# The output stage's row sums, reciprocals and first two batches prepared inside the attention stage, in GpSimd pieces of 512 columns

## The chip, the cores and the metric

One core of a Trainium2 chip runs the whole program in one launch. The metric is the device time of that launch in microseconds (us). The engines are TensorE (PE in the profile; PEld is its weight load), VectorE (DVE), ScalarE (ACT), GpSimd (POOL) and SyncE (SP), which here only issues DMA transfers.

## The reference

Four residual layers over x (4 batches x 512 rows x 512 columns), in float32:

```python
x = x + tanh(g_xattn[0]) * L0_xattn(layernorm(x), ctx, mask)         # one head, 1024 context rows
x = x + tanh(g_ffn[0])   * L0_ffn(layernorm(x), router, wg, wu, wd)  # 8 experts, quantized, top 1
x = x + tanh(g_xattn[1]) * L1_xattn(layernorm(x), ctx, Wq..bo)       # 16 heads of 32
x = x + tanh(g_ffn[1])   * L1_ffn(layernorm(x), w1, b1, w2, b2)      # 8 experts x 64 rows per batch
```

The change lies in the third layer. For each batch and each of 16 heads: scores = Q K^T / sqrt(32), softmax over 1024 context rows, context = softmax V; then `context @ Wo.T + bo`, the gate, the residual, and the layernorm and transposition that the last layer needs.

## The kernel before

The program is a row of stages, each a block of five instruction streams (one for each engine) with a barrier behind it: context, readout, router, mixture, query, attention, output, expert. Matmul operands are split into two bf16 halves (high and low), whose products are added up.

**Attention** (`attention_phase`) goes over 4 batches x 16 heads x 4 quarters u of 256 context rows; a quarter of a head is called a step here, 64 to a batch. The batch's step number is 4h+u. At a step TensorE issues eight matmuls of 512 columns: two that find a row maximum of a step 28 steps ahead (L1706, into `psM`, two slots), two for the scores 4 steps ahead (L1725), four that mix the values of this step (L1736). ScalarE takes the exponentials of those scores (L1632). Their low halves, 128x1024, are made by GpSimd for u = 0 and 2 (L1591) and by VectorE for u = 1 and 3 (L1678). VectorE also takes the maxima (L1670), so two steps of it are one low half and two maxima. The last batch has no maxima left to find from its step 36 on (head 9), and TensorE then has six matmuls a step. Once in 16 steps, at step number 5 modulo 16, GpSimd splits the maxima into three bf16 parts with four small instructions (`max_parts`, L1601 to L1607); TensorE transposes them four steps later (L1714) into a slot of `psM`. `copy_out` (L1646) takes a head's 96x512 sums, and SyncE stores them to `mixed_dram` (L1568): in it are, for each batch, two partial contexts (r = 0, 1) and the row sums of the softmax (r = 2).

**Output** (`output_phase`) does this for each batch of 128x2048 numbers: load both partial contexts (`load`, L1812), add them (L1900 on VectorE for batches 0 and 1, L1858 on GpSimd for 2 and 3), multiply by the reciprocal row sums (L1905), add the bias and split into halves (`high` L1868 on ScalarE, low L1908 on VectorE), project with Wo (L1970), update the residual `xres` and take statistics (L1915 to L1924), 1/sqrt on GpSimd (L1853), normalise (L1931), split (L1876, L1937), transpose (L1982), copy to `xeT` (L1881, L1943). The reciprocals need a way round: the row sums of all batches are loaded (L1821), inverted (L1949), stored to `rsum_dram` (L1827), and loaded again, each repeated over 32 partitions (`load_rsums`, L1817). GpSimd first adds the gated bias `bob` to all 16 rows of `xres` (L1848). VectorE goes through the batches in the order update, normalise, low half, divide(b+2), copy.

Everything on an engine runs in the order written; nothing is scheduled by a tool. Work on an engine waits for semaphores only, so the order within each stream is what the change moves.

## Time and profile before

| | us |
|---|---|
| median of 3 runs | 1772.18 (1770.33 to 1776.66) |
| the profiled execution | 1772.23, its span 1770.4 |
| attention, until the last copy of a head ends | to 1278.4 of the span |
| output stage, first DMA to last copy | 1284.84 to 1405.9 |
| expert stage | 1406 to the end |

The page's line for the span in 40 slices shows TensorE busy at nine tenths in attention (slices 20 to 28), at 2 and 6 to 5 tenths in the three slices after it, which are the output stage, and at nine tenths again in the expert stage:

```text
PE   4999988999551774878999999999826599999996
```

Times in the trace count from the span's start. A row of the timeline tells start, length, engine, line and operation, and in brackets how long the engine sat idle before it and what ended that. Several equal instructions in a row are merged, with their count behind an x.

### The profile page before, as it was taken

What the parts mean: (1) busy time and instruction counts of PE and PEld (TensorE: products, weight loads), DVE (VectorE), ACT (ScalarE), POOL (GpSimd) and SP (SyncE); (2) the same over time, 40 slices, a digit from 0 to 9 for tenths busy, and PEclk for the clock granted to TensorE, in tenths of its full rate; (3) what the DMA queues carried; (4) which work ended last, traced back from release to release, by engine and by line L of the source; (5) the groups of instructions that cost most, each with busy time, mean ns of one, the idle gap of its engine ahead of it and who ended that gap; (6) DMA issues with size and microseconds to landing.
All of it is one profiled execution on the core that took longest, in us unless ns stands there. A gap on an engine that the chain in (4) does not pass through costs nothing. (4 is left out here: it accounts for less than half of the span.)

```text
span 1770.4 us, 24758 instructions
## 1 busy us (share of the span) xinstructions
PE 1454.6 (82%) x8465; PEld 839.6 (47%) x8536; DVE 1258.1 (71%) x1520; ACT 970.7 (55%) x1440; POOL 438.6 (25%) x343
## 2 busy tenths in 40 slices
PE   4999988999551774878999999999826599999996
PEld 3554534555240333323555555555403366666663
DVE  4888856655582676859999999999448686655551
ACT  5878723344171555414777777767612376665551
POOL 0122210000313004304555555555752000000000
PEclk9999998999755996878999999999958699999998
DMA  6788650000083226420423233331177396666640
GB/s 220 244 276 290 204 205 1 0 0 0 1 354 111 72 90 186 111 79 11 97 74 95 76 92 79 90 81 28 36 213 226 115 327 219 219 220 219 220 142 28
DMA packets 145938, 236.92 MB, mean 134 GB/s; under 512 B 11320, under 2 KB 61496, under 8 KB 144704
## 3 DMA queue, kind: packets, MB, share of 16 engines
q1 hardware_dynamic: 140352, 210.65, 38.5%
q0 software_dynamic: 5504, 25.20, 3.9%
q8 instruction: 48, 0.79, 0.2%
q14 instruction: 34, 0.28, 0.1%
HBM read 169.74 MB, written 59.59 MB: 130 GB/s over the span
## 5 line engine op out<-in xcount | busy, mean ns | idle before, releaser
L1632 ACT ACTIVATE t_e<-t_psE 128x512 f32<-128x512 f32 x512 | 304.6, 597 | 133.6 <-PE t_psE L1725 124.9
L1670 DVE TENSOR_REDUCE t_nmax<-t_psM 128x1 f32<-128x1024 f32 x256 | 301.5, 1212 | 15.7 <-PE t_psM L1706 15.6
L1591 POOL TENSOR_TENSOR t_low<-t_e 128x1024 bf16<-128x1024 f32 x128 | 250.0, 1955 | 196.4 <-ACT t_e L1632 186.7
L1736 PE MATMUL t_psO<-t_e,vst 128*96 128x512 bf16 x512 | 200.6, 392 | 2.4 <-POOL t_low L1591 2.4
L1725 PE MATMUL t_psE<-qst,kst 99*128 99x512 bf16 x512 | 195.2, 382 | 0.1
L1736 PE MATMUL t_psO<-t_low,vst 128*96 128x512 bf16 x512 | 193.1, 377 | 0.0
L1678 DVE TENSOR_TENSOR t_low<-t_e 128x1024 bf16<-128x1024 f32 x128 | 177.9, 1390 | 18.3 <-ACT t_e L1632 17.8
L1706 PE MATMUL t_psM<-kst,qst 96*128 96x512 bf16 x512 | 164.0, 404 | 28.0 <-DVE t_nmax L1670 22.7
L2218 PE MATMUL e_psG<-xeT,e_w1p 128*128 (+1 forms) x1536 | 172.8, 276 | 9.4 <-DVE e_hT L2162 4.8
L2218 PEld LDWEIGHTS e_psG<-xeT,e_w1p 128*128 128x128 bf16 x1536 | 151.7, 99 | 30.9 <-issue 5.9
L2233 PE MATMUL e_psO<-e_w2p,e_hT 128*128 128x512 bf16 x752 | 164.9, 379 | 0.8
L2233 PEld LDWEIGHTS e_psO<-e_w2p,e_hT 128*128 128x128 bf16 x768 | 75.1, 98 | 88.9
L1736 PEld LDWEIGHTS t_psO<-t_e,vst 128*96 128x96 bf16 x512 | 84.1, 164 | 64.8 <-POOL t_low L1591 6.0
L1736 PEld LDWEIGHTS t_psO<-t_low,vst 128*96 128x96 bf16 x512 | 84.4, 165 | 27.4
L1706 PEld LDWEIGHTS t_psM<-kst,qst 96*128 96x128 bf16 x512 | 47.4, 99 | 94.0 <-DVE t_nmax L1670 47.2
L2114 ACT CAST e_w2p<-xres 128x2048 bf16<-128x2048 f32 x32 | 60.7, 1898 | 53.1 <-PE e_psO L2233 35.2
L642 PE MATMUL a_psR<-ctxN,a_pT 128*128 (+1 forms) x375 | 85.7, 384 | 4.3 <-DVE xres L555 3.9
L620 PE MATMUL a_psS<-ctxT,a_xT 128*128 (+1 forms) x375 | 87.8, 389 | 0.6 <-issue 0.2
L358 PE MATMUL c_psG<-ctxT,c_wT 128*128 128x512 bf16 x369 | 86.8, 383 | 1.0 <-issue 0.2
L115 POOL DMA_DIRECT2D ternary<-c_wout x48 | 41.7, 868 | 185.0 <-ACT c_wout L228 185.0
L2120 ACT ACTIVATE e_g<-e_psG,e_b1T 128x256 f32<-128x256 f32 x128 | 53.7, 470 | 59.5 <-PE e_psG L2218 40.7
L361 PE MATMUL c_psG<-c_wT,ctxT 128*128 128x512 bf16 x371 | 85.6, 379 | 0.7
(229 smaller groups left out, 2309.3 us busy)
## 6 DMA issues: line engine op xcount, KB each, us to landing
piece<-in_L_ffn_w SPq DMA_DIRECT2D x32, 1024.0 KB, 13.5
xres<-in_L_ffn_w SPq DMA_DIRECT2D x32, 1024.0 KB, 15.2
wT<-ternary POOLq DMA_DIRECT2D x8, 1536.0 KB, 21.4
kst<-keys SPq DMA_DIRECT2D x96, 128.0 KB, 4.2
mixed<-t_ost SPq DMA_DIRECT2D x64, 192.0 KB
c_rows<-in_ctx SPq DMA_DIRECT2D x8, 1024.0 KB, 10.3
xres<-in_L_ffn_wg SPq DMA_DIRECT2D x8, 1024.0 KB, 7.6
xres<-in_L_ffn_wu SPq DMA_DIRECT2D x8, 1024.0 KB, 7.1
```

What stands on the lines that cost most here:

```text
L358: last = nc.tensor.matmul(psG[:, k, :], wT[:, 0, a, k * P:(k + 1) * P], ctxT[:, b, q * 512:(q + 1) * 512], start=(i == 0), stop=(i == 11))
L620: last = nc.tensor.matmul(psS[:, par, h * 512:(h + 1) * 512], xT[:, par, ra * KC + k, :], ctxT[:, rb * KC + k, bass.ds(b * T + h * 512, 512)],
L642: last = nc.tensor.matmul(psR[:, :], pT[:, par, ra * TC + k, :], ctxN[:, bass.ds(b * TC + k, 1), rb, :].rearrange("p o d -> p (o d)"), sta ...
L1591: nc.gpsimd.tensor_tensor(low[:, slot(h, u), :, :], e32[:, slot(h, u), :, :], upper(h, u), ALU.subtract).then_inc(lo_pool, 1)
L1632: nc.scalar.activation(e32[:, slot(h, u), i, :], psE[:, i, :], ACT.Exp, scale=SC).then_inc(expd, 1)
L1670: nc.vector.tensor_reduce(nmax[:, h // G % 2, h % G, u:u + 1], banks_of(place_of_max(b, m)).rearrange("p a t -> p (a t)"), AX_X, ALU.max, ...
L1678: nc.vector.tensor_tensor(low[:, slot(h, u), :, :], e32[:, slot(h, u), :, :], upper(h, u), ALU.subtract).then_inc(lo_dve, 1)
L1706: last = nc.tensor.matmul(banks_of(place_of_max(b, m))[:, i, :], qst[0:KR, g, h % G, u * P:(u + 1) * P], kst[0:KR, g, h % G, i * 512:(i + ...
L1725: nc.tensor.matmul(psE[:, i, :], kst[:, g, h % G, k * P:(k + 1) * P], qst[:, g, h % G, :], start=True, stop=True).then_inc(scored, 1)
L1736: last = nc.tensor.matmul(psO[0:VW, h % 2, :], vst[:, g, 2 * u + i, :].rearrange("p (w h) -> p h w", h=G)[:, h % G, :], part[:, i, :], sta ...
L2218: last = nc.tensor.matmul(psG[:, g % 4, i, :], w1p[:, ra, k, f:f + P], xeT[:, rb * KC + k, ee, :].rearrange("p o s -> p (o s)"), start=(n ...
L2233: last = nc.tensor.matmul(psO[:, m, :], hT[:, ra, k, m * P:(m + 1) * P], w2p[:, rb, k, :], start=(k == 0 and i == 0), stop=(k == FC - 1 an ...
```

## The change

- **Batches 0 and 1 of the output stage** (PRE = 2) are prepared during the last batch of attention. SyncE loads their parts before the stores of heads 3 and 4; GpSimd adds the halves in eight pieces of 128x512, one behind each odd step of heads 4 to 7 (`add_halves`), and multiplies by the reciprocals in eight pieces behind each odd step of heads 9 to 12 (`divide`).
- **Reciprocals of batches 0 to 2**: sums loaded before the store of head 2, inverted by VectorE at step 20 of the last batch (48x512), stored before head 6's store, loaded repeated before those of heads 7 and 8. Batch 3's sums (16x512) stay in the output stage.
- **The gated bias**: loaded in batch 0, gated by VectorE at the start of batch 1, added to `xres` by GpSimd in 16 pieces of 128x512, at step numbers 5 and 13 modulo 16 of batches 1 and 2 (`bias_residual`).
- **The output stage** starts with `high` and `low` of batches 0 and 1. GpSimd adds the halves of batches 2 and 3 before its first 1/sqrt. Batches 2 and 3 have their own buffers.
- **Memory**: one allocation `prebob` holds the new buffers; the router's, query's and expert's tiles that were separate (`disp`, `qw32`, `xT`, `xeT`, `b2b`) are views of it.

The diff, cut to what the prediction speaks of:

```diff
+                def prepare_output(h):                                   # SyncE, last batch
+                    if h == 2:
+                        for i in range(2):
+                            sp.wait_ge(stored[i], 16 * (LAST * NH // 2 + 1))
+                        for b in range(LAST):
+                            load_sums(sp, b, o.sums[b * NH:(b + 1) * NH, :], mixed_dram, o.sums_loaded)
+                    if h in (3, 4):
+                        load_parts(sp, h - 3, o.pre[:, h - 3, :, :, :], mixed_dram, o.pre_loaded[h - 3])
+                    if h == 6:
+                        sp.wait_ge(o.rsums_ready, 1)
+                        sp.dma_start(o.rsum_dram[0:LAST].rearrange("b h s -> (b h) s"),
+                                     o.sums[:, :]).then_inc(o.rsums_stored, 16)
+                    if h in (7, 8):
+                        sp.wait_ge(o.rsums_stored, 16)
+                        sp.wait_ge(o.added, KC * (h - 6))
+                        load_rsums(sp, h - 7, o.pre[:, h - 7, 1, :, :], o.rsum_dram, o.rsum_loaded[h - 7])
...
                         if due := group_at(b, h, u, SPLIT_AT):            # GpSimd
                             max_parts(*due)
+                        if b in (1, 2) and h % 2 == 1 and u == 1:
+                            bias_residual((b - 1) * NH // 2 + h // 2)
+                        if b == LAST and 4 <= h < 8 and u % 2 == 1:
+                            add_halves((h - 4) // 2, (h % 2) * 2 + u // 2)
+                        if b == LAST and 9 <= h < 13 and u % 2 == 1:
+                            divide((h - 9) // 2, (h - 9) % 2 * 2 + u // 2)
...
+                    nc.gpsimd.tensor_tensor(o.xres[:, t, :], o.xres[:, t, :], o.bob[:, :], ALU.add).then_inc(o.biased, 1)
...
+                    pool.wait_ge(o.pre_loaded[b], 32)
+                    nc.gpsimd.tensor_tensor(o.pre[:, b, 0, k, :], o.pre[:, b, 0, k, :], o.pre[:, b, 1, k, :],
+                                            ALU.add).then_inc(o.added, 1)
...
+                    pool.wait_ge(o.rsum_loaded[b], 16 * (P // HD))
+                    pool.wait_ge(o.added, b * KC + k + 1)
+                    nc.gpsimd.tensor_tensor(o.pre[:, b, 0, k, :], o.pre[:, b, 0, k, :], o.pre[:, b, 1, k, :],
+                                            ALU.mult).then_inc(o.divided, 1)
...
+                def prepare_output(b, h, u):                              # VectorE
+                    if (b, h, u) == (1, 0, 0):
+                        dve.wait_ge(o.consts_loaded, 32)
+                        nc.vector.tensor_scalar(o.bob[:, :], o.bob[:, :], o.gates[:, 1:2], None, ALU.mult).then_inc(o.gated, 1)
+                    if (b, h, u) == (LAST, 5, 0):
+                        dve.wait_ge(o.sums_loaded, 16 * LAST)
+                        nc.vector.reciprocal(o.sums[:, :], o.sums[:, :]).then_inc(o.rsums_ready, 1)
...
+                load_sums(sp, LAST, sums[:, :], mixed_dram, sums_loaded)   # output stage, SyncE
+                for b in range(PRE, B):
+                    load_parts(sp, b, parts[:, b - PRE, :, :, :], mixed_dram, parts_loaded[b - PRE])
+                sp.wait_ge(rsums_ready, 1)
+                sp.dma_start(o.rsum_dram[LAST], sums[:, :]).then_inc(rsums_stored, 16)
+                sp.wait_ge(rsums_stored, 16)
+                for b in range(PRE, B):
+                    sp.wait_ge(added, b - PRE + 1)
+                    load_rsums(sp, b, parts[:, b - PRE, 1, :, :], o.rsum_dram, rsum_loaded[b - PRE])
...
-                pool.wait_ge(bo_gated, 1)                                 # output stage, GpSimd
-                for t in range(NT):
-                    nc.gpsimd.tensor_tensor(xres[:, t, :], xres[:, t, :], bob[:, :], ALU.add).then_inc(biased, 1)
+                for b in range(PRE, B):
+                    p = parts[:, b - PRE, :, :, :].rearrange("p r c s -> p r (c s)")
+                    pool.wait_ge(parts_loaded[b - PRE], 32)
+                    nc.gpsimd.tensor_tensor(p[:, 0, :], p[:, 0, :], p[:, 1, :], ALU.add).then_inc(added, 1)
...
-                divide(0)                                                 # output stage, VectorE
-                divide(1)
+                low(0)
+                low(1)
+                dve.wait_ge(sums_loaded, 16)
+                nc.vector.reciprocal(sums[:, :], sums[:, :]).then_inc(rsums_ready, 1)
```

GpSimd's stream over 16 steps of the last batch, before: eight low halves stand between two splits of the maxima.

```order
L1601 TENSOR_TENSOR t_nparts<-t_nmax,t_nparts 128x16
L1603 TENSOR_TENSOR t_nrest<-t_nmax,t_nparts 128x16
L1605 TENSOR_TENSOR t_nparts<-t_nrest,t_nparts 128x16
L1607 TENSOR_TENSOR t_nparts<-t_nrest,t_nparts 128x16
L1591 TENSOR_TENSOR t_low<-t_e 128x1024 x11
```

The same place after (`prebob` with L1690 is `divide`; the rows go on in this way up to the eighth piece and then `x4` low halves):

```order
L1649 TENSOR_TENSOR t_nparts<-t_nmax,t_nparts 128x16
L1651 TENSOR_TENSOR t_nrest<-t_nmax,t_nparts 128x16
L1653 TENSOR_TENSOR t_nparts<-t_nrest,t_nparts 128x16
L1655 TENSOR_TENSOR t_nparts<-t_nrest,t_nparts 128x16
L1690 TENSOR_TENSOR prebob<-prebob 128x512
L1639 TENSOR_TENSOR t_low<-t_e 128x1024
L1690 TENSOR_TENSOR prebob<-prebob 128x512
L1639 TENSOR_TENSOR t_low<-t_e 128x1024
```

A piece of 128x512 now stands ahead of each of seven low halves in the part of the batch that has no maxima, and the first stands between the split and the next low half. In batches 1 and 2 the pieces on `xres` are two for each eight low halves, the first again behind the split:

```order
L1655 TENSOR_TENSOR t_nparts<-t_nrest,t_nparts 128x16
L1680 TENSOR_TENSOR xres<-xres,prebob 128x512
L1639 TENSOR_TENSOR t_low<-t_e 128x1024 x4
L1680 TENSOR_TENSOR xres<-xres,prebob 128x512
L1639 TENSOR_TENSOR t_low<-t_e 128x1024 x4
```

VectorE around the start of the output stage, before (the first rows of the stage):

```order
L1678 TENSOR_TENSOR t_low<-t_e 128x1024 x13
L1550 UNCONDITIONAL_BRANCH
L1893 UNCONDITIONAL_BRANCH
L1947 TENSOR_SCALAR o_bob<-o_bob,gates 128x512
L1949 RECIPROCAL o_sums<-o_sums 64x512
L1900 TENSOR_TENSOR o_parts<-o_parts 128x2048
L1905 TENSOR_TENSOR o_parts<-o_parts 128x2048
L1908 SCALAR_TENSOR_TENSOR o_cpair<-o_parts,o_bias,o_cpair 128x512 x4
```

and after:

```order
L1749 TENSOR_TENSOR t_low<-t_e 128x1024 x13
L1573 UNCONDITIONAL_BRANCH
L1953 UNCONDITIONAL_BRANCH
L1965 SCALAR_TENSOR_TENSOR o_cpair<-prebob,o_bias,o_cpair 128x512 x8
L2006 RECIPROCAL o_sums<-o_sums 16x512
L1972 SCALAR_TENSOR_TENSOR xres<-o_psG,gates,xres 128x512
```

The sums, the four full-width instructions of batches 0 and 1 and the gating are gone from in front of the low halves; a reciprocal stands between the low halves and the first update.

## Rows read from the trace of the kernel before

**Rows 1.** Windows, busy us and (count) by engine, then clock, DMA share, GB/s.

```profile
1050.00:1160.00 110.00, 104.84 (x478) 61.68 (x477) 106.25 (x90) 78.14 (x137) 63.82 (x46) 1.00 0.36 89
1240.00:1278.00 38.00, 35.35 (x153) 20.93 (x151) 20.68 (x12) 29.43 (x54) 32.01 (x16) 1.00 0.14 37
1278.00:1406.00 128.00, 57.73 (x316) 30.18 (x320) 84.66 (x116) 27.42 (x41) 38.35 (x23) 0.71 0.56 170
```

**Rows 2.** Timeline of the output stage, by start: SyncE, VectorE, TensorE.

```profile
1284.84 1.95 SPq L1821 DMA_DIRECT2D o_sums<-mixed  x4
...
1292.38 3.34 DVE L1949 RECIPROCAL o_sums<-o_sums 64x512 f32<-64x512 f32 x1
...
1310.34 2.29 DVE L1905 TENSOR_TENSOR o_parts<-o_parts 128x2048 f32<-128x2048 f32 x1 [10.72 <-DMA o_parts<-rsum]
...
1318.78 21.97 PE L1970 MATMUL o_psG<-woT,o_cpair 128*128 128x512 bf16 x94 [40.98 <-DVE o_cpair L1908]
...
1323.64 2.74 DVE L1908 SCALAR_TENSOR_TENSOR o_cpair<-o_parts,o_bias,o_cpair 128x512 bf16<-128x512 f32 x4 [0.79 <-ACT o_cpair L1868]
```

**Rows 3.** Timeline of attention, GpSimd, just behind a split of maxima and in the repeating part.

```profile
1214.35 1.89 POOL L1591 TENSOR_TENSOR t_low<-t_e 128x1024 bf16<-128x1024 f32 x1
...
1226.06 1.89 POOL L1591 TENSOR_TENSOR t_low<-t_e 128x1024 bf16<-128x1024 f32 x1 [1.63 <-ACT t_e L1632]
1229.58 1.89 POOL L1591 TENSOR_TENSOR t_low<-t_e 128x1024 bf16<-128x1024 f32 x1 [1.63 <-ACT t_e L1632]
```

**Rows 4.** The same stretch on VectorE and TensorE.

```profile
1215.76 1.57 DVE L1678 TENSOR_TENSOR t_low<-t_e 128x1024 bf16<-128x1024 f32 x1
1217.24 1.21 DVE L1670 TENSOR_REDUCE t_nmax<-t_psM 128x1 f32<-128x1024 f32 x1
...
1220.67 1.23 DVE L1678 TENSOR_TENSOR t_low<-t_e 128x1024 bf16<-128x1024 f32 x1 [0.28 <-ACT t_e L1632]
...
1225.44 2.34 DVE L1670 TENSOR_REDUCE t_nmax<-t_psM 128x1 f32<-128x1024 f32 x2
1227.71 1.32 DVE L1678 TENSOR_TENSOR t_low<-t_e 128x1024 bf16<-128x1024 f32 x1
...
1218.51 0.60 PE L1706 MATMUL t_psM<-kst,qst 96*128 96x512 bf16 x2 [1.32 <-DVE t_nmax L1670]
...
1227.33 0.59 PE L1706 MATMUL t_psM<-kst,qst 96*128 96x512 bf16 x2
```

**Rows 5.** Line L1848, GpSimd's add of 128x512: minimum, median, maximum in ns.

```profile
L1848 POOL TENSOR_TENSOR xres<-xres,o_bob x16: 1255/1256/3315, 1292.5 to 1315.4; 128x512 f32<-128x512 f32 x16
```

**Rows 6.** Timeline of attention's last steps, without maxima: GpSimd, VectorE, TensorE.

```profile
1252.45 7.60 POOL L1591 TENSOR_TENSOR t_low<-t_e 128x1024 bf16<-128x1024 f32 x3 [1.16 <-DVE t_low L1678]
1261.22 7.60 POOL L1591 TENSOR_TENSOR t_low<-t_e 128x1024 bf16<-128x1024 f32 x3 [1.16 <-DVE t_low L1678]
...
1258.32 4.06 DVE L1678 TENSOR_TENSOR t_low<-t_e 128x1024 bf16<-128x1024 f32 x2 [1.87 <-ACT t_e L1632]
...
1275.78 0.47 PE L1736 MATMUL t_psO<-t_e,vst 128*96 128x512 bf16 x1 [0.82 <-POOL t_low L1591]
```

**Rows 7.** Timeline of the output stage, VectorE and GpSimd, one batch after another.

```profile
1326.29 0.74 DVE L1915 SCALAR_TENSOR_TENSOR xres<-o_psG,gates,xres 128x512 f32<-128x512 f32 x1
...
1333.59 6.12 DVE L1931 TENSOR_SCALAR o_xn<-xres,o_mom,o_rstd 128x512 f32<-128x512 f32 x4 [1.20 <-POOL o_rstd L1853]
...
1333.70 4.81 POOL L1858 TENSOR_TENSOR o_parts<-o_parts 128x2048 f32<-128x2048 f32 x1
...
1350.46 0.74 DVE L1915 SCALAR_TENSOR_TENSOR xres<-o_psG,gates,xres 128x512 f32<-128x512 f32 x1
...
1374.61 0.74 DVE L1915 SCALAR_TENSOR_TENSOR xres<-o_psG,gates,xres 128x512 f32<-128x512 f32 x1
...
1381.90 1.92 DVE L1931 TENSOR_SCALAR o_xn<-xres,o_mom,o_rstd 128x512 f32<-128x512 f32 x4 [1.20 <-POOL o_rstd L1853]
```

**Rows 8.** DMA issues from 1150 to 1410 us: KB each, median us from issue to landing.

```profile
o_parts<-mixed SPq DMA_DIRECT2D x8, 1024.0 KB, 8.3
```

More of the change, by code:

```diff
@@ L1 @@
+from collections import namedtuple
 from contextlib import ExitStack
@@ L1433, in _, with load_parts, load_rsums, load_sums @@
                     gemm(b)
-def attention_phase(nc, queries_dram, keys_dram, values_dram, mixed_dram, ident, qst, loaded, kst, vst, kv_loaded, ones_set):
+Output = namedtuple("Output", "pre sums bob bias rsum_dram gates xres bv bo consts_loaded sums_loaded pre_loaded rsum_loaded "
+                              "gated rsums_ready rsums_stored added divided biased")
+PRE = 2
+def load_parts(sp, b, target, mixed_dram, loaded):
+    for r in range(2):
+        sp.dma_start(target[:, r, :, :], mixed_dram[b, r].rearrange("(c p) s -> p c s", p=P)).then_inc(loaded, 16)
+def load_rsums(sp, b, target, rsum_dram, loaded):
+    rsum_v = rsum_dram.rearrange("b (c g) s -> b g c s", g=P // HD)
+    for g in range(P // HD):
+        sp.dma_start(target[g * HD:(g + 1) * HD, :, :],
+                     rsum_v[b:b + 1, g].to_broadcast([HD, KC, S])).then_inc(loaded, 16)
+def load_sums(sp, b, target, mixed_dram, loaded):
+    sp.dma_start(target, mixed_dram.rearrange("b r (h d) s -> b r h d s", d=HD)[b, 2, :, 0, :]).then_inc(loaded, 16)
+def attention_phase(nc, queries_dram, keys_dram, values_dram, mixed_dram, ident, qst, loaded, kst, vst, kv_loaded, ones_set, o):
     SC = float(HD) ** -0.5
@@ L1776, in output_phase @@
         sem = lambda name: c.enter_context(nc.semaphore(name))
-        parts = sb("o_parts", [P, 2, 3, KC, S], F32)
-        sums = sb("o_sums", [B * NH, S], F32)
-        bias = sb("o_bias", [P, KC], F32)
-        bob = sb("o_bob", [P, D], F32)
+        parts = sb("o_parts", [P, B - PRE, 2, KC, S], F32)
+        sums = sb("o_sums", [NH, S], F32)
         cpair = sb("o_cpair", [P, 2, 2, KC, S], BF16)
@@ L1795, in output_phase @@
         rsum_loaded = [sem(f"o_rsum_loaded{i}") for i in range(2)]
-        bo_gated, biased = sem("o_bo_gated"), sem("o_biased")
-        summed, added, divided = sem("o_summed"), sem("o_added"), sem("o_divided")
+        added, divided = sem("o_added"), sem("o_divided")
         c_hi, c_lo = sem("o_c_hi"), sem("o_c_lo")
@@ L1803, in output_phase, with quotient @@
         stored = sem("o_stored")
+        def quotient(b):
+            return o.pre[:, b, 0, :, :] if b < PRE else parts[:, b - PRE, 0, :, :]
         with nc.Block() as block:
@@ L1863, in high @@
                 def high(b):
-                    act.wait_ge(divided, b + 1)
+                    if b < PRE:
+                        act.wait_ge(o.divided, KC * (b + 1))
+                    else:
+                        act.wait_ge(divided, b - PRE + 1)
                     if b >= 2:
@@ L1957, in _ @@
                         divide(b + 2)
+                        low(b + 2)
                     x_copy(b)
@@ L1990, in _, with expert_phase @@
                     transposes(b)
-def expert_phase(nc, w1, b1, w2, b2, ident, x3_dram, gates, xeT, piece, w1_loaded, xres, out):
+def expert_phase(nc, w1, b1, w2, b2, ident, x3_dram, gates, xeT, piece, w1_loaded, xres, b2b, out):
     F = w1.shape[2]
@@ L2316, in prefetch_queries @@
                     load_queries(sp, 0, g, queries_dram, qst, q_loaded)
+            late_sem = lambda name: late.enter_context(nc.semaphore(name))
+            o = Output(pre=pre, sums=dsums, bob=bob, bias=bias, rsum_dram=rsum_dram, gates=gates, xres=xres,
+                       bv=a["L1_xattn_bv"], bo=a["L1_xattn_bo"], consts_loaded=late_sem("o_consts_loaded"),
+                       sums_loaded=late_sem("o_dsums_loaded"), pre_loaded=[late_sem(f"o_pre_loaded{i}") for i in range(PRE)],
+                       rsum_loaded=[late_sem(f"o_drsum_loaded{i}") for i in range(PRE)], gated=late_sem("o_gated"),
+                       rsums_ready=late_sem("o_drsums_ready"), rsums_stored=late_sem("o_drsums_stored"),
+                       added=late_sem("o_pre_added"), divided=late_sem("o_pre_divided"), biased=late_sem("o_biased"))
             query_phase(nc, place, gates, mixture_dram, qw32, qw_loaded, a["L1_xattn_bq"], queries_dram, ident, xres, woT,
-                        kst, vst, ones_set, prefetch, prefetch_queries)
+                        kst, vst, ones_set, prefetch, prefetch_queries, columns)
             attention_phase(nc, queries_dram, keys_dram, values_dram, mixed_dram, ident, qst, q_loaded, kst, vst, kv_loaded,
-                            ones_set)
-        xeT = late.enter_context(nc.sbuf_tensor("xeT", [P, 2 * KC, E, B * S // E], BF16))
+                            ones_set, o)
+        xeT = prebob[:, 0:PRE * PW].bitcast(BF16).rearrange("p (k e s) -> p k e s", k=2 * KC, e=E)
         F = a["L1_ffn_w1"].shape[2]
```

100 lines of the change are left out of this document (39 added, 61 removed).

## The prediction

> **What bounds the kernel now.** I read the stages first (windows), then the timeline of the output stage, then that of attention. Their rows say two things. In the 128 us of the output stage TensorE is busy for 58 and no other engine for more than 85, with the DMA engines at 0.56: it is a chain of waits, not a load [rows 1]. Attention has almost no air: in 110 us TensorE is busy 105 and VectorE 106, while GpSimd is busy 64 and looks like the place to put work [rows 1]. The expert stage behind both starts when the output stage ends, and the change leaves it as it is.
>
> In the output stage, call its first DMA T0, 1284.84. Sums, constants and parts are loaded, the reciprocal comes at 1292.38, the first division only at 1310.34 after 10.7 us of waiting for the repeated reciprocals, and TensorE starts at 1318.78, 33.9 us behind T0 [rows 2]. Then each batch is one round on VectorE: updates start at 1326.29, 1350.46 and 1374.61, and the stage ends at 1405.9, 121.1 behind T0 [rows 7].
>
> **A shared resource in attention.** GpSimd's low half takes 1.89 us beside VectorE's maxima, which are not stretched either (2.34 for two) [rows 3, 4]. Where VectorE does low halves instead, both suffer: three of GpSimd's take 7.60 and start 8.77 apart, two of VectorE's take 4.06 where one alone takes 1.23 [rows 4, 6]. 3 x 1.89 leaves 3.10 of 8.77 for three VectorE halves, 1.03 each: they exclude each other, and the last part of attention is exactly their sum. The 128x512 add shows it too: 1.256 usually, 3.315 once, about one 2.29 us VectorE instruction more [rows 5, 2]. So a GpSimd piece is free only beside maxima, a reciprocal or idle time.
>
> **The change, part by part.** Profiled execution 1772.23, median 1772.18: nothing to convert.
>
> *1. Sixteen bias pieces in batches 1 and 2.* VectorE is nearly full: two maxima and a low half are 2.34 + 1.23 less 0.1 to 0.2 of overlap, in a period of 3.52 [rows 3, 4]. A piece comes right behind a GpSimd low half, when VectorE's (1227.71) already waits and goes first. The piece then runs to about 1230.2, GpSimd's next low half (due 1229.58) ends at 1232.1, and VectorE's next (due 1231.23) is about 0.65 late. TensorE needs VectorE's maximum, done at 1226.6, only at 1227.33, so it has 0.7 us of lead and loses nothing; some 0.1 is made up every two steps [rows 3, 4]. That holds for the 8 pieces at step number 13. The 8 at number 5 stand behind the split of the maxima. There the chain is tight: GpSimd's low half at 1214.35 ends at 1216.24, VectorE's is stretched to 1.57 by it, the maximum at 1217.24 follows and TensorE waits 1.32 for it until 1218.51 [rows 3, 4]. A piece in front of this low half passes 1.26 straight through. 8 x 1.26 = **+10.1**. Bounds: 0 if pieces find the idle 1.63, 20 if all sixteen cost 1.26. Gating `bob` (0.5 of VectorE, once) goes into the lead.
>
> *2. Adds and a reciprocal in heads 4 to 7 of the last batch.* Eight pieces, one every two steps. The exclusive work is then 1.89 + 1.13 + 1.26 = 4.28 per two steps against 3.52: +0.76, in seven of the eight pairs +5.3. In the eighth the 3.34 us reciprocal stands between maxima; GpSimd runs beside it, as it did beside the one of 64x512 (not stretched: its median was 1.256), so that pair costs +3.3 and hides its piece. One wait of 1.3 at a split is swallowed, and 0.7 of lead is used up. **+6.6**; bounds 2.6 (reciprocal less lead) and 13.4 (8 x 1.26 + 3.3) [rows 2, 4, 5].
>
> *3. Divisions in heads 9 to 12.* Here the end of attention is the chain of exclusive work, TensorE waiting 0.82 for GpSimd at its last step [rows 6]. 8 x 1.256 = **+10.0**; bounds 5 (some of it into waits for exponentials, up to 1.87 on VectorE) and 12.6 (at 1.57 apiece, the mean with waits) [rows 5, 6].
>
> *4. Transfers moved.* SyncE now issues 3 + 4 loads before heads 2 to 4 and 1 + 8 before heads 6 to 8. Behind them in its queue stand the store of a head, which ScalarE needs two heads (14 us) later, and the rows of maxima after heads 4 and 8, due two heads later: covered. It also waits at head 8 for the eighth add, a few us, with 7 until the next store. Two 1 MB loads land after 8.3 us [rows 8]; the first piece is reached about 9.5 us behind their issue, so **0**; a load 4 us slower would make GpSimd stand for up to 3.
>
> *5. The output stage.* Low(0) ends 0.79 + 2.74 = 3.5 behind T0 and TensorE starts there instead of at 33.9 [rows 2]. The clock granted in the stage was 0.71 before as well, and a start after a pause runs at the low level in both. 96 matmuls take 22.4, batch 0's half about 12, so its last tile is ready at 15.7. VectorE does low(1) to 6.2, the 16x512 reciprocal (same 512 columns, 3.34) to 9.6, updates until 17.7. But GpSimd is now busy: parts of batch 2 land at about 9.5, its 4.81 us add ends at 14.4; batch 3's land at about 17, the add ends at 22.3; only then comes the 1/sqrt, and normalise starts at 23.5, not 18.8 [rows 7, 8]. From normalise to the next update there were 16.87 us, of which the 4.2 that 6.12 has over 1.92 were spent behind GpSimd's add; that add is gone from there. Update(1) at 23.5 + 12.7 = 36.1. The next round, 24.15, also loses 4.2: update(2) at 56.1. From there to the end 31.3 as before, with transpositions that wait for TensorE: 87.4 instead of 121.1. Repeated reciprocals (batch 2 by about 22, batch 3 by about 30) are earlier than their divisions. **-33.7**; bounds -26 (batch 3's parts 8 us later) and -38 (1/sqrt not held up) [rows 2, 7].
>
> Sum: 10.1 + 6.6 + 10.0 - 33.7 = -7.0, **1765.2 us**.
>
> **Rivals.**
> A, slower: *VectorE has no lead to give*. The lead of 0.7 and the gain of 0.1 per pair are read off one pattern. If GpSimd gets its turn first each time, VectorE's low half waits 1.26 for each of the 24 pieces that stand between maxima, and TensorE with it: 24 x 1.26 + 3.3 + 10.0 = 43.6 - 33.7 = +10, 1782. The change is worth nothing from a mean price of (33.7 - 3.3 - 10.0) / 24 = 0.85 us for such a piece. For: both engines over 95% [rows 1]. Against: VectorE's half is already waiting when the piece arrives (1227.71 against 1227.95), and maxima run unstretched beside GpSimd [rows 3, 4].
> The Trainium skill stands on this rival's side: Perfetto Trace Analysis, § Optimizing Scalar/DVE Operations, warns that work moved between VectorE and GpSimd may gain nothing, since they share a read port, and SBUF — State Buffer, § Who interferes with whom, that the one that starts second is blocked for the other's whole instruction. Taken strictly, all the exclusive work of the 24 pieces would be added to a full VectorE, which is A's 1782 and not 1765. The trace agrees with the blocking (7.60 for 5.67 of work), but whether a piece falls beside maxima or in front of a low half is what decides here, and the page's exception for reductions is what the unstretched 2.34 shows.
> B, *the pieces are free while maxima are there*: 1.26 fits GpSimd's idle 1.63 [rows 3]. Cost 2.6 + 10.0 only: -21, 1751. Against: rows 6.
> C, *the gain is smaller than the chain says*, or a load is late where GpSimd waits for it: batch 3's parts 8 us later, everything else as above, gives +1, 1773; with the first piece's load late 3 more. It is also how the change could fail to do what it says: prepared batches that are ready, behind a GpSimd that is not. For: GpSimd's queue is now in the middle of the stage. Against: the two 1 MB parts landed in 8.3 us each, so two pairs in 17 us is what that row gives [rows 8].
>
> **How the numbers follow.** Forecast 0.60 (spread 4.5 either way), A 0.12, B 0.13, C 0.15. A measurement of this kernel tells about 0.3% from no change, 5.3 us. Of the forecast 0.38 lies below -5.3, 0.21 within, 0.01 above; B is all faster; C 0.13 within and 0.02 above; A slower. Faster 0.51, same 0.34, slower 0.15. The range holds the forecast with its bounds, B's and C's: 1751 to 1777; A is left out.
>
> **What would show it.** Step 1: TensorE's wait for VectorE's maximum behind a split grows from 1.3 to about 2.6 in batches 1 and 2, and elsewhere in them it hardly waits; the two batches are 10 us longer. Step 2: a period of 4.3 in heads 4 to 7. Step 3: low halves of GpSimd followed by pieces of 1.26 without idle time, and the last TensorE wait still on GpSimd. Step 5: projection about 3.5 behind the first DMA of the stage, VectorE waiting some 5 us for the first 1/sqrt, no 6.12 on the normalise lines, the stage about 87 us. It would be wrong if VectorE's low halves in attention do not move (B), or if TensorE waits at step 13 as well (A).

## The result, and the profile after

The changed kernel takes 1764.04 us (median of 20 runs, 1760.33 to 1776.80) against 1772.63 (20 runs, 1767.03 to 1777.78): a ratio of 0.9964, 95% interval 0.9948 to 0.9980. The ratio is estimated from all the runs; their means are 1766.3 and 1772.9, while the two medians alone would give 0.9952. The kernel is faster by 0.2 to 0.5%. The forecast was 1765.2, with a range of 1751 to 1777.

**The ledger.** The first instruction of each split of the maxima on GpSimd (L1649 after, L1601 before) comes once in 16 steps and can serve as a milestone. The four that matter, after:

```profile
802.13 0.21 POOL L1649 TENSOR_TENSOR t_nparts<-t_nmax,t_nparts 128x16 bf16<-128x16 f32 x1 [20.02 <-DVE t_nmax L1741]
...
919.22 1.20 POOL L1649 TENSOR_TENSOR t_nparts<-t_nmax,t_nparts 128x16 bf16<-128x16 f32 x1
...
1197.89 0.22 POOL L1649 TENSOR_TENSOR t_nparts<-t_nmax,t_nparts 128x16 bf16<-128x16 f32 x1
...
1263.95 1.20 POOL L1649 TENSOR_TENSOR t_nparts<-t_nmax,t_nparts 128x16 bf16<-128x16 f32 x1
```

Their counterparts before start at 798.40, 915.49, 1182.60 and 1241.69. With the first DMA of the output stage (1316.42 after; 1284.84 before, [rows 2]) the differences are:

| stretch, us | before | after | change | predicted |
|---|---|---|---|---|
| nine periods with the pieces of batches 1 and 2 (from 915.49) | 267.11 | 278.67 | +11.6 | +10.1 |
| two periods with heads 4 to 7 of the last batch (from 1182.60) | 59.09 | 66.06 | +7.0 | +6.6 |
| last split to output stage | 43.15 | 52.47 | +9.3 | +10.0 |
| output stage, to the end of the last copy | 121.1 | 83.8 | -37.3 | -33.7 |
| sum | | | -9.4 | -7.0 |

The two profiled spans differ only by 3.6 (1770.4 and 1766.8): the first split came 3.7 us later, and the expert stage took 2 us more. The first split lies between 793.7 and 802.1 in all the profiles of this study, and before's 798.4 is in the middle of them, so this part is taken for the spread from run to run. For the expert stage that is less sure: from the last copy to the end of the span it takes 364.5 us in the one profile of before and 365.3 to 368.4 in the ten profiles of changed kernels. No run shows whether that is the change (its buffers lie elsewhere in memory) or chance.

The windows of after, in the columns of [rows 1]: a stretch in the middle of attention, the last steps, the output stage.

```profile
1053.00:1163.00 110.00, 102.81 (x468) 60.66 (x467) 106.65 (x88) 76.34 (x134) 71.53 (x48) 1.00 0.33 80
1264.00:1316.40 52.40, 34.11 (x144) 19.63 (x142) 24.09 (x12) 28.45 (x51) 41.95 (x23) 0.97 0.11 30
1316.40:1400.20 83.80, 57.25 (x316) 29.26 (x320) 65.75 (x111) 26.70 (x40) 13.19 (x7) 0.81 0.52 176
```

TensorE's 57 us of the output stage are the same work as before, now in 84 us instead of 121 (the window of [rows 1] also holds the end of attention). In the middle of attention it lost 2 of its 105 busy us, while GpSimd got 8 us of extra work.

**Behind a split of the maxima**, GpSimd, then VectorE, then TensorE, in batch 1:

```profile
984.13 0.21 POOL L1655 TENSOR_TENSOR t_nparts<-t_nrest,t_nparts 128x16 bf16<-128x16 f32 x1
984.31 1.27 POOL L1680 TENSOR_TENSOR xres<-xres,prebob 128x512 f32<-128x512 f32 x1
985.54 1.89 POOL L1639 TENSOR_TENSOR t_low<-t_e 128x1024 bf16<-128x1024 f32 x1
...
985.88 2.63 DVE L1749 TENSOR_TENSOR t_low<-t_e 128x1024 bf16<-128x1024 f32 x1
...
957.26 0.60 PE L1787 MATMUL t_psM<-kst,qst 96*128 96x512 bf16 x2 [2.52 <-DVE t_nmax L1741]
...
989.70 0.60 PE L1787 MATMUL t_psM<-kst,qst 96*128 96x512 bf16 x2 [2.40 <-DVE t_nmax L1741]
```

The piece stands ahead of the low half, VectorE's low half (985.88) grows to 2.63, and TensorE waits 2.40 where it waited 1.29 (1.32 in [rows 4]). This comes eight times in batches 1 and 2, and no other wait of TensorE for a maximum there is over 1 us. At step 13 the piece (968.31, 2.25) waits itself and costs nothing:

```profile
968.31 2.25 POOL L1680 TENSOR_TENSOR xres<-xres,prebob 128x512 f32<-128x512 f32 x1
...
971.63 1.87 DVE L1749 TENSOR_TENSOR t_low<-t_e 128x1024 bf16<-128x1024 f32 x1
```

**Heads 4 to 7 and the last steps.** Low halves of GpSimd are 4.29 apart beside the adds (3.5 in [rows 3]), and 4.07 beside the divisions, where the period was 8.77 / 3 = 2.92 [rows 6]; there TensorE waits 1.18 in each pair:

```profile
1242.45 1.89 POOL L1639 TENSOR_TENSOR t_low<-t_e 128x1024 bf16<-128x1024 f32 x1 [1.16 <-DVE t_low L1749]
1244.30 1.28 POOL L1684 TENSOR_TENSOR prebob<-prebob 128x512 f32<-128x512 f32 x1
1246.74 1.89 POOL L1639 TENSOR_TENSOR t_low<-t_e 128x1024 bf16<-128x1024 f32 x1 [1.16 <-DVE t_low L1749]
...
1276.33 1.89 POOL L1639 TENSOR_TENSOR t_low<-t_e 128x1024 bf16<-128x1024 f32 x1
1278.18 2.26 POOL L1690 TENSOR_TENSOR prebob<-prebob 128x512 f32<-128x512 f32 x1
1280.40 1.89 POOL L1639 TENSOR_TENSOR t_low<-t_e 128x1024 bf16<-128x1024 f32 x1
...
1277.10 2.20 DVE L1749 TENSOR_TENSOR t_low<-t_e 128x1024 bf16<-128x1024 f32 x1 [1.87 <-ACT t_e L1703]
...
1278.27 0.47 PE L1817 MATMUL t_psO<-t_e,vst 128*96 128x512 bf16 x1 [1.18 <-POOL t_low L1639]
```

**The output stage** (T0 = 1316.42), the rows that answer to [rows 2] and [rows 7]:

```profile
1317.26 5.39 DVE L1965 SCALAR_TENSOR_TENSOR o_cpair<-prebob,o_bias,o_cpair 128x512 bf16<-128x512 f32 x8 [11.66 <-ACT o_cpair L1928]
1322.56 3.33 DVE L2006 RECIPROCAL o_sums<-o_sums 16x512 f32<-16x512 f32 x1
1325.82 0.64 DVE L1972 SCALAR_TENSOR_TENSOR xres<-o_psG,gates,xres 128x512 f32<-128x512 f32 x1
...
1325.37 4.52 POOL L1911 TENSOR_TENSOR o_parts<-o_parts 128x2048 f32<-128x2048 f32 x1 [8.84 <-DMA o_parts<-mixed]
1330.73 4.51 POOL L1911 TENSOR_TENSOR o_parts<-o_parts 128x2048 f32<-128x2048 f32 x1 [0.83 <-DMA o_parts<-mixed]
1333.97 1.29 DVE L1981 TENSOR_SCALAR o_veps<-o_mom 128x4 f32<-128x4 f32 x1
...
1335.42 1.02 POOL L1916 TENSOR_TENSOR o_rstd<-o_veps,o_half 128x4 f32<-128x4 f32 x1 [0.17 <-DVE o_veps L1981]
...
1336.47 1.92 DVE L1988 TENSOR_SCALAR o_xn<-xres,o_mom,o_rstd 128x512 f32<-128x512 f32 x4 [1.20 <-POOL o_rstd L1916]
...
1348.93 0.74 DVE L1972 SCALAR_TENSOR_TENSOR xres<-o_psG,gates,xres 128x512 f32<-128x512 f32 x1
```

### The profile page after: what moved, and what is told of

It is laid out like the page before. It is cut to its first block and busy times, and to the rows that moved or that the text cites. A ratio compares the mean times of both kernels' runs of the same rounds, so it can differ in the third digit from the quotient of the medians.

```text
span 1766.8 us, 24778 instructions
## 1 busy us (share of the span) xinstructions
PE 1456.9 (82%) x8465; PEld 838.0 (47%) x8536; DVE 1261.2 (71%) x1517; ACT 970.0 (55%) x1440; POOL 467.0 (26%) x359
## 5 line engine op out<-in xcount | busy, mean ns | idle before, releaser
L1639 POOL TENSOR_TENSOR t_low<-t_e 128x1024 bf16<-128x1024 f32 x128 | 244.1, 1908 | 172.6 <-ACT t_e L1703 122.5
L1749 DVE TENSOR_TENSOR t_low<-t_e 128x1024 bf16<-128x1024 f32 x128 | 195.0, 1523 | 23.7 <-ACT t_e L1703 23.4
L2273 PE MATMUL e_psG<-prebob,e_w1p 128*128 (+1 forms) x1536 | 171.9, 275 | 12.6 <-DVE e_hT L2217 7.8
L2273 PEld LDWEIGHTS e_psG<-prebob,e_w1p 128*128 128x128 bf16 x1536 | 150.9, 98 | 34.0 <-issue 8.0
L1787 PEld LDWEIGHTS t_psM<-kst,qst 96*128 96x128 bf16 x512 | 46.9, 100 | 111.5 <-DVE t_nmax L1741 66.2
L116 POOL DMA_DIRECT2D ternary<-c_wout x48 | 45.4, 945 | 181.9 <-ACT c_wout L229 181.9
```

Source lines behind the costliest of these rows:

```text
L1639: nc.gpsimd.tensor_tensor(low[:, slot(h, u), :, :], e32[:, slot(h, u), :, :], upper(h, u), ALU.subtract).then_inc(lo_pool, 1)
L1749: nc.vector.tensor_tensor(low[:, slot(h, u), :, :], e32[:, slot(h, u), :, :], upper(h, u), ALU.subtract).then_inc(lo_dve, 1)
L1787: last = nc.tensor.matmul(banks_of(place_of_max(b, m))[:, i, :], qst[0:KR, g, h % G, u * P:(u + 1) * P], kst[0:KR, g, h % G, i * 512:(i + ...
L2273: last = nc.tensor.matmul(psG[:, g % 4, i, :], w1p[:, ra, k, f:f + P], xeT[:, rb * KC + k, ee, :].rearrange("p o s -> p (o s)"), start=(n ...
```

## The experiments

All stretches in this table are measured between the same milestones. "Attention" is from the first split to the start of the output stage. The groups of runs were made on different chips, where before took 1772.6, 1771.7, 1775.5 and 1774.7 us, so stretches and ratios can be compared better than medians.

| kernel | batches 1, 2 | heads 4 to 7 | last steps | attention | median, us | ratio to before |
|---|---|---|---|---|---|---|
| before | 267.1 | 59.1 | 43.2 | 486.4 | 1772.6 | 1 |
| after | 278.7 | 66.1 | 52.5 | 514.3 | 1764.0 | 0.9964 |
| bias pieces at steps 1 and 9 | 269.0 | 66.3 | 52.4 | 504.9 | 1753.3 | 0.9896 |
| bias pieces at steps 9 and 13 | 267.2 | 66.1 | 52.4 | 502.9 | 1754.6 | single run |
| no bias pieces | 268.0 | 66.2 | 52.4 | 503.7 | 1749.4 | single run |
| fills for the adds | 278.7 | 62.6 | 52.5 | 510.9 | 1763.4 | single run |
| divisions on VectorE | 277.1 | 66.4 | 46.3 | 506.8 | 1756.9 | 0.9919 |
| both moves | 269.1 | 66.5 | 46.3 | 498.9 | 1750.0 | 0.9870 |
| spread | 269.4 | 59.0 | 48.0 | 493.6 | 1741.9 | 0.9821 |
| spread, again | 269.2 | 59.1 | 47.2 | 492.6 | 1740.8 | 0.9802 |
| spread, loads split | 269.5 | 59.1 | 45.9 | 491.5 | 1738.3 | 0.9803 |

**1. Which bias pieces cost.** In one kernel the pieces stand at steps 1 and 9 modulo 16 instead of 5 and 13:

```diff
-                        if b in (1, 2) and h % 2 == 1 and u == 1:
+                        if b in (1, 2) and h % 2 == 0 and u == 1:
```

> The changed kernel with its 16 bias pieces at step numbers 1 and 9 modulo 16 of batches 1 and 2 instead of 5 and 13; nothing else. Theory (a piece costs only where it stands between a split of the maxima and the next low half): 16 steps take 29.7 to 30.0 us again instead of 30.8 in these batches, attention is 7 to 9 us shorter than in the changed kernel, about 1756. Rival (each piece costs its exclusive time wherever it stands): still 30.8, no difference. Rival (the pieces cost nothing and the 1.1 us come from elsewhere, the longer program or the transfers): still 30.8.

In a second they are left out, with the wait for them; the gated bias is then missing from the result:

```diff
-                        if b in (1, 2) and h % 2 == 1 and u == 1:
-                            bias_residual((b - 1) * NH // 2 + h // 2)
...
-                        dve.wait_ge(o.biased, t + 1)
```

> The changed kernel without the 16 bias pieces: the addition of the gated bias to the residual is left out of the computation. Theory: every 16 steps of batches 1 and 2 take 29.68 us as before the change, all but the one with the gating instruction (up to 1.7 more, once); attention 10 to 11.5 us shorter than in the changed kernel. Rival (transfers or memory layout slow attention): periods stay above 30.

In a third only the eight pieces at step 5 moved, to step 9:

```diff
-                        if b in (1, 2) and h % 2 == 1 and u == 1:
-                            bias_residual((b - 1) * NH // 2 + h // 2)
+                        if b in (1, 2) and h % 4 >= 2 and u == 1:
+                            bias_residual((b - 1) * NH // 2 + h // 4 * 2 + h % 4 - 2)
```

> The changed kernel with only the eight bias pieces of step number 5 moved, to step number 9; the eight at step number 13 stay. Theory (a piece at 13 is absorbed by the 0.7 us of lead, one at 5 passes its length on): 16 steps of batches 1 and 2 take 29.7 to 29.9 us. Rival (a step of 29.8 in the run with pieces at 1 and 9 came from moving the second piece too): 30.2 or more.

Measured: 269.0, 268.0 and 267.2 us for batches 1 and 2, against 278.7 after. The sixteen pieces cost 278.7 - 268.0 = 10.7. Moving eight of them takes all of it away (267.2, even 0.8 less than with no pieces). So the eight at step 5 carry the whole price. A piece at step 9 or 13 costs nothing, and sixteen at steps 1 and 9 cost 1.0 us together (269.0 against 268.0), 0.06 each. With pieces at 1 and 9 the waits behind the splits are back at 1.41:

```profile
979.85 0.60 PE L1787 MATMUL t_psM<-kst,qst 96*128 96x512 bf16 x2 [1.41 <-DVE t_nmax L1741]
```

The time was 1753.32 (1750.97 to 1754.41, 4 runs), a ratio of 0.9896, interval 0.9873 to 0.9919. The kernel without pieces and the one with pieces at 9 and 13, each run once, gave 1749.44 and 1754.55. Rival A of the prediction (every piece costs) is out, and so is B (none does).

The Trainium skill's rule in SBUF — State Buffer, § Who interferes with whom, that the later of two contending instructions stands for the other's whole length, agrees with the rows above: the piece of 1.26 takes 2.25 behind a VectorE half (968.31). But it says what a single instruction suffers, not what the kernel pays; that was 1.1 us or nothing, by place.

**2. Where in the queue, or on the shared resource?** The eight adds of heads 4 to 7 are replaced by fills of 128x1280, which take GpSimd nearly as long but read nothing. The halves of batches 0 and 1 are not added in this kernel:

```diff
-                    nc.gpsimd.tensor_tensor(o.pre[:, b, 0, k, :], o.pre[:, b, 0, k, :], o.pre[:, b, 1, k, :],
-                                            ALU.add).then_inc(o.added, 1)
+                    nc.gpsimd.memset(o.pre[:, b, 1, :, :].rearrange("p c s -> p (c s)")[:, 0:1280], 0.0).then_inc(o.added, 1)
```

> The changed kernel with the eight adds of heads 4 to 7 replaced by GpSimd memsets of 128x1280 float32, which only write and should take about as long (1.2 to 1.3 us): the addition of the two partial contexts of batches 0 and 1 is left out of the computation. Theory (VectorE's low half and a GpSimd instruction that reads exclude each other, so that two steps take 1.89 + 1.13 + 1.26 = 4.28): with a fill that does not exclude, VectorE's low halves stay at 1.2 to 1.3 and two steps take 3.52 to 3.6 again, 5 to 6 us less over these heads. Rival (GpSimd's time alone, or any GpSimd instruction, blocks): the period stays about 4.3.

Measured, GpSimd and VectorE:

```profile
1242.36 1.17 POOL L1686 MEMSET prebob<- 128x1280 f32 x1
1244.05 1.89 POOL L1639 TENSOR_TENSOR t_low<-t_e 128x1024 bf16<-128x1024 f32 x1 [0.52 <-ACT t_e L1704]
1245.88 1.17 POOL L1686 MEMSET prebob<- 128x1280 f32 x1
...
1242.17 1.32 DVE L1750 TENSOR_TENSOR t_low<-t_e 128x1024 bf16<-128x1024 f32 x1
```

GpSimd's low halves are 3.52 apart again with 1.17 us of work between them, and VectorE's are not stretched (1.32 against 2.10). Heads 4 to 7 take 62.6: 3.4 less than after (5 to 6 were expected), 3.5 more than before. So here the time in GpSimd's queue was free, and what cost was that the adds read operands while VectorE wanted to. The 3.5 that are left are put down to the reciprocal of 3.33 us on VectorE by elimination: beside the fills the period is before's 3.52, and the spread kernel below, which has neither the adds nor the reciprocal in this stretch, takes 59.0. The miss of the expectation shows in the rows of after: only the last four adds lengthen a period to 4.28, 4 x 0.77 = 3.1, while the first four stand around the reciprocal and the split and add little. The sentence of the Trainium skill (SBUF — State Buffer, § Who interferes with whom) that VectorE's two-input instructions contend with a GpSimd instruction that reads SBUF and not with one that only writes it is what these rows show.

**3. The divisions on VectorE.** They stand behind the same steps' low halves:

```diff
-                        if b == LAST and 9 <= h < 13 and u % 2 == 1:
-                            divide((h - 9) // 2, (h - 9) % 2 * 2 + u // 2)
...
+                    if b == LAST and 9 <= h < 13 and u % 2 == 1:
+                        quotient((h - 9) // 2, (h - 9) % 2 * 2 + u // 2)
...
+                    nc.vector.tensor_tensor(o.pre[:, b, 0, k, :], o.pre[:, b, 0, k, :], o.pre[:, b, 1, k, :],
+                                            ALU.mult).then_inc(o.divided, 1)
```

> The changed kernel with the eight division pieces of heads 9 to 12 on VectorE, which idles there, instead of GpSimd. A 128x512 two-input instruction should take VectorE about 0.6 us (a quarter of 2.29) against 1.26. Theory (the last part of attention is the sum of what the two engines do under mutual exclusion): the divisions cost 8 x 0.6 = 4.8 instead of 9.3 to 10, so 4.5 to 5.5 us shorter than the changed kernel, about 1759. Rival (only GpSimd's own queue is full): they cost nothing, 9 to 10 us shorter, about 1754. Rival (VectorE delays its low halves by each piece and these bind): no gain.

Measured: 46.3 instead of 52.5 for the last steps, 6.2 shorter where 4.5 to 5.5 were expected and 9 to 10 by the rival, 1756.87 us (1750.60 to 1760.21), ratio 0.9919 (0.9892 to 0.9945). The period, read on GpSimd's low halves, is 3.44:

```profile
1263.48 0.68 DVE L1771 TENSOR_TENSOR prebob<-prebob 128x512 f32<-128x512 f32 x1
...
1263.63 2.27 POOL L1639 TENSOR_TENSOR t_low<-t_e 128x1024 bf16<-128x1024 f32 x1 [1.16 <-DVE t_low L1741]
...
1267.07 2.27 POOL L1639 TENSOR_TENSOR t_low<-t_e 128x1024 bf16<-128x1024 f32 x1 [1.16 <-DVE t_low L1741]
```

In the exclusive chain a piece costs about what it holds the resource: 4.07 - 2.92 = 1.15 on GpSimd, 3.44 - 2.92 = 0.52 on VectorE, where the instruction takes 0.68. Over all eight it was 3.1 us (46.3 - 43.2), as some of them stand ahead of the last split or in idle time. The busy shares of these steps point the same way, other than those of the middle of attention: in the last 52.4 us of after (the second window above) GpSimd is busy 42.0 and VectorE 24.1, and VectorE waits 1.87 for an exponential before each low half. Its idle time did not make the pieces free, though.

**4. Both moves together**, to see whether they add up:

> Bias pieces at step numbers 1 and 9 and the divisions on VectorE together. If the two savings lie on separate stretches of one chain they add: 9.4 + 5.8 = 15 us below the changed kernel, about 1749; if they hide behind one another, 1753.

Measured: 1749.98 us (1747.26 to 1755.76), ratio 0.9870 (0.9839 to 0.9901). Attention is 498.9, 15.4 less than after; one by one they gave 9.4 and 7.5. They add up, except for 1.5, for which the last section has the likely reason.

**5. Every piece where it has cover.** The adds go to batch 2, at steps 1 and 9, in the place of half the bias pieces. The bias for the rows of batches 2 and 3 is added in the output stage, by GpSimd beside VectorE's updates. The reciprocal is cut into four of 128 columns, in head 9, and the divisions stand in heads 13 and 15:

```diff
+                        if b == 1 and h % 2 == 0 and u == 1:              # GpSimd
+                            bias_residual(h // 2)
+                        if b == 2 and h % 2 == 0 and u == 1:
+                            add_halves(h // 8, h // 2 % 4)
...
+                    if b in (1, 2):                                       # output stage, GpSimd
+                        pool.wait_ge(odd_copied, 2 * b)
+                        for t in range((b + 1) * QD, (b + 2) * QD):
+                            nc.gpsimd.tensor_tensor(xres[:, t, :], xres[:, t, :], o.bob[:, :], ALU.add).then_inc(o.biased, 1)
...
+                    if (b, h) == (LAST, 9):                               # VectorE
+                        dve.wait_ge(o.sums_loaded, 16 * LAST)
+                        c = slice(u * P, (u + 1) * P)
+                        nc.vector.reciprocal(o.sums[:, c], o.sums[:, c]).then_inc(o.rsums_ready, 1)
+                    if b == LAST and h in (13, 15):
+                        quotient((h - 13) // 2, u)
...
+                    if h == 10:                                           # SyncE, last batch
+                        sp.wait_ge(o.rsums_ready, 4)
...
+                        for b in range(PRE):
+                            sp.wait_ge(o.added, KC * (b + 1))
+                            load_rsums(sp, b, o.pre[:, b, 1, :, :], o.rsum_dram, o.rsum_loaded[b])
```

> As v1_both, and: the eight adds at step numbers 1 and 9 of batch 2 (their loads before the stores of head 12 of batch 1 and head 3 of batch 2); bias pieces of batches 0 and 1 in batch 1, those of batches 2 and 3 in the output stage beside VectorE's updates, which read PSUM and one SBUF operand; the reciprocals in four pieces of 128 columns in head 9 of the last batch, where VectorE idles; the divisions on VectorE in heads 13 and 15. Theory: all but about 1 us for the gating, 16 x 0.06 and 2 to 3 for the divisions goes away, so attention is 4 to 5 us longer than before the change instead of 27.9, and the output stage stays at 83 to 84: about 1741. Rival (updates do exclude GpSimd, or the late divisions are waited for): output stage 5 or more us longer, about 1747.

Measured: 1741.89 us (1740.92 to 1748.74), ratio 0.9821 (0.9793 to 0.9849). Heads 4 to 7 are back at 59.0, which is before's time. Attention is 493.6, 7.1 longer than before where 4 to 5 were expected. The output stage still takes 83.8, with the bias in it (82.0 to 83.8 in the kernels without), and the updates beside it are not stretched:

```profile
1323.68 4.94 POOL L1921 TENSOR_TENSOR xres<-xres,prebob 128x512 f32<-128x512 f32 x4 [12.66 <-DVE prebob L2007]
...
1324.90 0.73 DVE L1979 SCALAR_TENSOR_TENSOR xres<-o_psG,gates,xres 128x512 f32<-128x512 f32 x1
```

The update reads one of its two large operands from PSUM, and beside GpSimd's adds it takes 0.73, as without them (0.73 to 0.74 in the later batches of after). But the last steps took 48.0 and not the 46.3 of the kernel before it. ScalarE's copy of a head waited for its buffer, whose last store (of head 10) stood behind the eight loads of 256 KB in SyncE's order, and TensorE waited for ScalarE:

```profile
1266.91 0.58 ACT L1711 COPY t_ost<-t_psO 96x512 f32<-96x512 f32 x1 [3.78 <-DMA mixed<-t_ost]
...
1268.05 0.61 PE L1809 MATMUL t_psE<-qst,kst 99*128 99x512 bf16 x1 [3.77 <-ACT t_e L1697]
...
1248.32 0.32 SPq L1595 DMA_DIRECT2D rsum<-o_dsums  x1
1253.41 3.64 SPq L1450 DMA_DIRECT2D prebob<-rsum  x8
1257.10 28.26 SPq L1618 DMA_DIRECT2D mixed<-t_ost  x6
```

SyncE's rows show that the bytes of the loads need not be all of it. Head 10 was copied by 1252.0, but its store was issued at 1257.10, 5.1 us later: until 1253.41 SyncE waited for the store of the reciprocals, and then it took 3.64 to issue the eight loads.

**6. Is that wait the order of the loads?** The first four loads stand before the store of head 11, the other four before that of head 13:

```diff
+                    if h in (11, 13):
+                        b = (h - 11) // 2
                         sp.wait_ge(o.rsums_stored, 16)
-                        for b in range(PRE):
-                            sp.wait_ge(o.added, KC * (b + 1))
-                            load_rsums(sp, b, o.pre[:, b, 1, :, :], o.rsum_dram, o.rsum_loaded[b])
+                        sp.wait_ge(o.added, KC * (b + 1))
+                        load_rsums(sp, b, o.pre[:, b, 1, :, :], o.rsum_dram, o.rsum_loaded[b])
```

> The same work as in the spread version; only SyncE's order in the last batch differs. There the eight loads of repeated reciprocals (2 MB) stood in one row before the store of head 10, behind a wait for the store of the reciprocals; the store of that head came 3.8 us too late for ScalarE's copy, TensorE stood 3.77 us and then ran at a granted clock of 0.72 and 0.60 for 10 us. Here the first four loads stand before head 11's store and the second four before head 13's. Theory (the row of 2 MB caused the wait, and the wait the fall of the clock): ScalarE's wait for the store is under 1 us, the clock stays at 1.00 through the last steps, attention from the first split of the maxima to the start of the output stage takes about 4 to 5 us less than the 493.6 of the spread version, so 489, and the time is about 1737 to 1738. Rival 1 (any load of this kind in the last heads makes a store late, whatever its size): the wait comes twice, 2 us each, and the time stays at 1742. Rival 2 (the wait goes, but what comes next, the exclusive work of low halves, was as long anyway): under 1.5 us shorter, 1740 to 1741.

> The spread version again, unchanged, on the chip of the split one, so that 4 us can be told apart from the difference between chips. Its attention is expected at 493.6 us as before, with the wait of 3.8 us for the store and the fall of the granted clock behind it, if both are a property of the order of transfers; if they were an accident of one execution, the wait is absent here, and the split version gains nothing over it.

Measured: the spread version again waits 3.83 for the store, so it is a property of the order. In the split one no engine waits for a store in the last steps, and the clock stays at 1.00 there. This version takes two things from in front of head 10's store at once, the wait for the reciprocals' store and the loads, and which of them made it late no run separates. Its time is 1738.29 (1735.15 to 1742.08), ratio 0.9803 (0.9782 to 0.9823); the spread version beside it 1740.84 (1736.08 to 1744.52), ratio 0.9802 (0.9783 to 0.9822). Attention is only 1.1 shorter (491.5 and 492.6), and the two times can't be told apart. The wait went with the order, but the gain was not the 4 to 5 us expected: rival 2 came true. Without the pause the chain of exclusive work is next, VectorE's divisions among the low halves, and TensorE waits for GpSimd's:

```profile
1260.72 4.68 DVE L1775 TENSOR_TENSOR prebob<-prebob 128x512 f32<-128x512 f32 x2
...
1266.62 2.28 POOL L1642 TENSOR_TENSOR t_low<-t_e 128x1024 bf16<-128x1024 f32 x1 [1.76 <-DVE t_low L1744]
...
1273.51 0.47 PE L1821 MATMUL t_psO<-t_e,vst 128*96 128x512 bf16 x1 [1.54 <-POOL t_low L1642]
```

The first two divisions take 4.68 here and took 2.98 in the spread version. Both versions beat the changed kernel (their intervals lie below its 0.9948) and before, by about 2.0% or 35 us.

## Why the prediction was right

**The sum.** -7.0 was forecast; the ledger has -9.4, and the means of the runs differ by 6.6. The errors of the steps partly cancel, which is luck: attention cost 1.2 more than predicted and the output stage gave 3.6 more.

**What bounds the kernel.** Confirmed: the output stage was a chain of waits. Taking 37 of its 121 us away left TensorE's 57 as they were. Attention had no air: it grew by 27.9, where 26.7 were predicted.

**Step 1, bias pieces, +10.1; measured +11.6.** The mechanism was right in detail: pieces at step 5 pass through, pieces at step 13 are absorbed, TensorE's wait grows from 1.3 to "about 2.6" (2.40 measured). The eight waits cost 8 x 1.11 = 8.9 instead of 10.1. Two terms were missing, and that 10.1 still came near 11.6 is in part luck. The granted clock fell behind one of the eight waits, +1.8 (last section). And the gating of `bob` was put at nothing: it took 1.66 us instead of the 0.49 that it takes alone, because GpSimd's low half had begun 0.5 earlier, and batches 1 and 2 are 0.9 longer than before even with no bias pieces:

```profile
940.00 1.89 POOL L1639 TENSOR_TENSOR t_low<-t_e 128x1024 bf16<-128x1024 f32 x1 [1.63 <-ACT t_e L1703]
...
940.52 1.66 DVE L1769 TENSOR_SCALAR prebob<-prebob,gates 128x512 f32<-128x512 f32 x1
```

The prediction looked at the contention of two-input instructions only. The Trainium skill, SBUF — State Buffer, § Who interferes with whom, lists `tensor_scalar` among those that can contend as well, and these rows agree.

**Step 2, adds and reciprocal, +6.6; measured +7.0.** The period is 4.29, 4.28 was said. By the fills, 3.4 of the 7.0 are the adds and 3.5, by elimination, the reciprocal (predicted 3.3 for that pair). The prediction let the reciprocal's pair hide its piece and swallowed one wait at a split; together that was nearly what happened.

**Step 3, divisions, +10.0; measured +9.3.** Low halves and pieces on GpSimd follow each other without idle time, and the last wait of TensorE is 1.49, on GpSimd, as said. A piece cost 1.15, not 1.256.

**Step 4, transfers, 0.** A small miss in the case of one load: the first add waited 1.71 for its parts. The two prefetches of 1 MB took a median of 9.4 us, with stores and loads of sums in the same queue, against the 8.3 of [rows 8] that the step was built on. How much of the 1.71 was paid, with 1.63 of idle time at this place anyway, no run isolates:

```profile
1222.16 1.28 POOL L1684 TENSOR_TENSOR prebob<-prebob 128x512 f32<-128x512 f32 x1 [1.71 <-DMA prebob<-mixed]
```

**Step 5, the output stage, -33.7; measured -37.3.** The term that failed is the 1/sqrt behind GpSimd's second add. The prediction had that add end at T0 + 22.3 and normalise start at 23.5. It ended at 18.8, and normalise started at 20.05: with four loads issued in one row, the second pair of parts was there 5.4 us after the first, not 8. The 8.3 of [rows 8] is one load's time from issue to landing, and the prediction read it as the spacing of the two pairs. So VectorE waited for the 1/sqrt by 1.2 only and not by the 5 expected (the add still cost about 1.1: beside it the small instruction of L1981 took 1.29, and 0.17 in the later batches); update(1) came at 32.5 instead of 36.1, and that 3.6 is the whole miss. The round after it took 19.3, where 20.0 were said, and the normalise lines take 1.92 and no longer 6.12.

**Rivals.** A would have needed waits at step 13; there are none over 1 us. B would have needed TensorE's waits behind a split to stay at 1.3. C expected parts later than 17 us, and they came earlier.

## What to carry to other kernels

The price of small work put on an idle engine is not its own time but where it stands: the same 1.26 us piece cost 0, 0.4, 1.1 or 1.15 us, by whether VectorE, which it excludes, has slack there or is busy with what it doesn't exclude; look for the chain that is tight and place pieces outside it. Prepare a stage early only as far as the earlier stage has such places, and put the rest beside instructions of the stage itself that don't contend. Where everything on the path is exclusive, a piece costs about as long as it holds the shared resource, so the engine that is faster at it is the cheaper place; idle time on either engine does not by itself make it free.
